# Attention with a gated output projection: VectorE or GpSimd adds the output bias to x

## The chip, the cores and the metric

The kernel runs on one core of one Trainium2 chip. The metric is the device time of one execution in microseconds; the figure compared is the median of several executions. The core has TensorE (PE in the profile), VectorE (DVE), ScalarE (ACT), GpSimd (POOL) and SyncE (SP, here the queue that issues the DMAs).

## What is computed

A model of four layers works on x, 32 sequences of 128 tokens with 128 features in float32. Each layer adds a gated attention and a gated feed-forward to x. Attention has 16 heads of 8 features; queries come from the normalised x, keys and values from a context of the same shape:

```python
x = x + tanh(g_xattn[0]) * attn0(layernorm(x), ctx, mask)
x = x + tanh(g_ffn[0])   * ffn0(layernorm(x))          # fp8 weights and activations
x = x + tanh(g_xattn[1]) * attn1(layernorm(x), ctx)    # ends in  heads @ Wo.T + bo
x = x + tanh(g_ffn[1])   * ffn1(layernorm(x))          # 8 experts, top 2
x = x + tanh(g_xattn[2]) * attn2(layernorm(x), ctx)    # heads attend within one token
x = x + tanh(g_ffn[2])   * ffn2(layernorm(x))
x = x + tanh(g_xattn[3]) * attn3(layernorm(x), ctx, mask)  # ends in  heads @ Wo.T + bo
x = x + tanh(g_ffn[3])   * ffn3(layernorm(x))          # 8 experts, top 2
```

Only layers 1 and 3 have an output projection `Wo` with a bias `bo`. The kernel computes `x + tanh(g) * (heads @ Wo.T)` and adds `tanh(g) * bo`, which is laid out once in `tgbo`, in a second step.

## The kernel before, in words

**Tiles and stages.** x stays in SBUF throughout, as 32 tiles of 128 tokens by 128 features; a tile is one sequence. Four tiles make a group (TG = 4), so there are 8 groups. The kernel is written by hand, engine by engine: every engine has its own program, and semaphores tie them together. The stages follow one another: attention block a = 0, feed-forward 0, attention block a = 1 (layer 1), feed-forward 1, the token attention of layer 2 mixed into it, feed-forward 2, attention block a = 2 (layer 3), feed-forward 3. The start of a block (`start=True`) is mixed into the stage ahead of it.

**Loops.** `walk` (L288) runs a stage's body over the groups: groups 0 and 1 unrolled, groups 2 to 5 in a hardware loop of two trips, groups 6 and 7 unrolled.

**One attention block.** For tile n TensorE writes scores in four banks of four heads (`scores`, L854 the mask, L856 the products), and VectorE takes the row maxima (`head_max`, L1225). Score bank j waits for the maxima of bank j - 2, because only two banks take turns. VectorE splits the maxima in two bf16 parts (L1247, L1249), TensorE turns them (L866), ScalarE copies them (L663), TensorE makes the transposed scores (L875, L879), ScalarE the exponentials (L670), and TensorE weighs the values (L891). The heads are turned (L903), divided by their denominators on VectorE (L1256, L1258), turned again (L908) and multiplied with Wo (L912). The result stands in R_BANK.

**The work around the change.** On VectorE the order inside tile n (all for tile n + 1 or n - 1) is written out by hand in `body`: row maxima of n + 1 (banks 0 and 1), `normalise(n - 1)`, banks 2 and 3, `split_max(n + 1)`, then `add_out(n - 1)`. In the first tile of a group `norm_stats` (L1176, L1181) and `norm` (L1199) of the group after next follow, in the second tile the bias of v (`take_v`, L1210) stands ahead of the row maxima. `add_out` waits for R_BANK, adds gate times R_BANK to x (L1266), waits for that instruction's own semaphore, and adds `tgbo` (L1270), which signals `x_written`.

GpSimd's program in a block (L478 and on) has, per group: `inv_std` for the group after next (L439, L441: variance to rstd, for which VectorE's `norm` waits) and `split` of that group's queries and keys into three bf16 parts (L450, L452, L455). When the split is ready SyncE issues the DMAs that spread the parts over `q_rows` and `k_rows` (L355, L359). `x_written` of a block is waited for by the next stage: by TensorE before its first matmuls, and by VectorE's `norm_stats` for the group at hand.

Of the kernel before, what the change touches and what calls it, by code (L numbers as in the profile page):

```python
# [37 lines left out]
ALU = mybir.AluOpType  # L38
# [3 lines left out]
P = 128  # L42
NT = 32
TG = 4
# [34 lines left out]
def waits_apart(eng):  # L79

    eng.nop(nofuse=True)
# [23 lines left out]
def program(nc, x_in, ctx_in, ctx_t, mask0, mask3, w_attn, w_ffn0, w_router, w_gate, w_up, w_down, w1, w2, gate3,  # L105
            mlp1, mlp2, mlp2_b, cols_in, rows_in, consts_in, pick_in, out):
    with ExitStack() as ctx:  # L107
        def sb(name, shape, dt=F32):
            return ctx.enter_context(nc.sbuf_tensor(name, shape, dt))
# [15 lines left out]
        gates = sb("gates", [P, 8])  # L125
        half_gates = sb("half_gates", [P, 2, 8])
        tgbo = sb("tgbo", [P, 2, P])
# [82 lines left out]
        R_BANK = bank[5]  # L210
# [28 lines left out]
        def tile(n):  # L239
            return x[:, bass.ds(n * P, P)]  # L240
# [16 lines left out]
        R0 = (0, NT, 4 * NT)  # L257
        BLOCK = (0, 2, 5)
        LAYER = (0, 1, 3)
# [28 lines left out]
        def walk(eng, body, chain=None, per_trip=None, after_first=None):  # L288


            body(0, True, False)
            if after_first:
                after_first()
            if chain is not None:
                chain.enter(0, per_trip)
                chain.count = chain.base
            with eng.Fori(0, NG // 2 - 2) as trip:
                if chain is not None:
                    chain.count = chain.base + trip * per_trip
                body(2 + 2 * trip, False, False)  # L300
            if chain is not None:
                chain.leave(NG // 2 - 2)
            body(NG - 2, False, True)
# [4 lines left out]
        def groups(gp, first, last):  # L308

            for b in range(2):  # L310
                yield gp + b, b, first and b == 0, (1 - b if last else 2)
# [3 lines left out]
        def _(sp):  # L315
# [88 lines left out]
            def token_attention():  # L404
                def body(gp, first, last):
                    for gr, b, _, _ in groups(gp, first, last):
                        if positive(TG * (gr - 1)):
                            sp.wait_ge(ctx_tok_read, TG * (gr - 1))
                        waits_apart(sp)
                        sp.dma_start(ctx_tok[b][:], ctx_in[bass.ds(gr * TG, TG)].rearrange("n p d -> p n d")  # L410
                                     ).then_inc(ctx_tok_loaded[b], 16)
                walk(sp, body)
# [18 lines left out]
        def _(pool):  # L431
# [3 lines left out]
            def inv_std(count):  # L435

                pool.wait_ge(stats_ready, count)
                waits_apart(pool)
                pool.tensor_scalar(rstd_a[:], meanvar[:, :, 1], LN_EPS, None, ALU.add).then_inc(pool_steps, ch.one())  # L439
                pool.wait_ge(pool_steps, ch.count)  # L440
                pool.tensor_tensor(rstd[:], rstd_a[:], minus_half[:, 0:TG], ALU.pow).then_inc(rstd_ready, 1)  # L441

            def split(p, a):

                pool.wait_ge(prep_read, 4 * (G0[a] + p) + 3)
                pool.wait_ge(rows_spread, REP * (G0[a] + p))
                for part in range(2):
                    src = qk if part == 0 else qk_rest
                    waits_apart(pool)
                    pool.tensor_copy(parts[:, :, part, :], src).then_inc(pool_steps, ch.one())  # L450
                    pool.wait_ge(pool_steps, ch.count)
                    pool.tensor_tensor(qk_rest, src, parts[:, :, part, :], ALU.subtract).then_inc(pool_steps, ch.one())  # L452
                    pool.wait_ge(pool_steps, ch.count)
                waits_apart(pool)
                pool.tensor_copy(parts[:, :, 2, :], qk_rest).then_inc(split_ready, 1)  # L455
# [20 lines left out]
                walk(pool, body, ch, 12)  # L476

            def attention(a):  # L478
                def body(gp, first, last, a=a):
                    for gr, b, _, left in groups(gp, first, last):  # L480
                        if left >= 2:
                            inv_std(L0[a] + gr + 3)
                            split(gr + 2, a)
                walk(pool, body, ch, 10)

            def feed_forward3():
                def products(k, e):
# [114 lines left out]
            def feed_forward2():  # L602
# [17 lines left out]
                for count in range(46, 51):  # L620
                    inv_std(count)

            todo = (attention0, feed_forward0, lambda: attention(1), feed_forward1_and_tokens,
                    feed_forward2, lambda: attention(2), feed_forward3)
            for step in todo[:PHASES]:
                step()
# [3 lines left out]
        def _(act):  # L630
# [92 lines left out]
            def feed_forward0():  # L723
                def body(gp, first, last):
                    for gr, b, _, _ in groups(gp, first, last):
                        take_turned(0, gr, b)
                walk(act, body, after_first=lambda: attention(1, True))
# [34 lines left out]
            def feed_forward2():  # L762
                take_turned(2, 0, 0)

                def body(gp, first, last):
                    for gr, b, _, left in groups(gp, first, last):
                        for m in range(4):
                            act.wait_ge(hq_filled, 4 * gr + m + 1)
                            act.wait_ge(down_filled, DB2 + gr)
                            waits_apart(act)  # L770
                            act.activation(hq[:, m, :], bank[m][:], ACT.Relu, bias=cols[:, C_B1 + m:C_B1 + m + 1],
                                           saturate=False).then_inc(hq_ready, 1)
                        if left >= 1:
                            take_turned(2, gr + 1, 1 - b)
                        if first:
                            token_exp(NT - TG + b)
                walk(act, body, after_first=lambda: attention(2, True))
# [364 lines left out]
        def _(dve):  # L1142
# [60 lines left out]
            def attention(a, start):  # L1203
# [59 lines left out]

                def add_out(n, a=a):
                    dve.wait_ge(r_filled, R0[a] + 3 * n + 3)
                    ins = dve.scalar_tensor_tensor(tile(n), R_BANK[:, 0:P], gates[:, LAYER[a]:LAYER[a] + 1], tile(n),  # L1266
                                                   ALU.mult, ALU.add)
                    ins.then_inc(r_read, 1)
                    dve.wait_ge(r_read, R0[a] + 3 * n + 3)
                    dve.tensor_tensor(tile(n), tile(n), tgbo[:, a - 1, :], ALU.add).then_inc(x_written, 1)  # L1270

                xc = NT * BLOCK[a]
                if start:
# [36 lines left out]
                def body(gp, first, last, a=a, xc=xc):  # L1310
                    for gr, b, is_first, left in groups(gp, first, last):
                        for t in range(TG):
# [18 lines left out]
                            if has_prev and a > 0:  # L1331
                                add_out(n - 1)
# [12 lines left out]
                if a > 0:  # L1345
                    add_out(NT - 1)
# [387 lines left out]
```

## Time and profile before

| | |
|---|---|
| Three runs, median | 1875.36 us |
| Three runs, lowest and highest | 1872.49 and 1875.47 us |
| The profiled execution, its own time | 1866.39 us |
| Its span, first to last instruction | 1864.6 us |
| TensorE matmuls busy | 1517.3 us, 81% |
| TensorE weight loads busy | 920.6 us, 49% |
| VectorE busy | 1345.4 us, 72% |
| ScalarE busy | 780.6 us, 42% |
| GpSimd busy | 642.2 us, 34% |
| Mean granted TensorE clock | 0.918 |

The busy shares are means over stages that differ in their limits. The two blocks that the edit touches are the stretches from about 403 to 635 us and from about 1365 to 1595 us. Times in the timeline are microseconds from the first instruction. "[2.91 <-DVE neg_max L1225]" behind an instruction says that its engine had stood idle for 2.91 us before it, and what released it. An execution in the loop is told from an unrolled one by its shapes, which the profile then gives once and not as output<-input.

### The profile page before, as it was taken

The page shows a single profiled execution, that of the slowest core. Times are in us where ns is not written, and L with a number is a line of the kernel's source. Part 1 is how long each engine was busy: PE and PEld are TensorE (multiplying, and loading weights), DVE is VectorE, ACT ScalarE, POOL GpSimd, SP SyncE. Part 2 cuts the span into 40 slices and gives each one's busy share as a digit, 9 for nine tenths or more (in the row PEclk, how much of TensorE's full clock was granted, in tenths as well). Part 3 has the DMA queues.
Part 4 walks back from the last instruction along what each step waited for, and adds up shares of the span by engine and source line. Part 5 has one row for each costly group of instructions (what it writes and reads, how often), then busy time and mean ns, then how long its engine had stood idle before and what let it go on. Part 6 is the DMA issues. An engine that isn't in the chain of part 4 may idle for free. (4 is left out here: it accounts for less than half of the span.)

```text
span 1864.6 us, 33511 instructions
## 1 busy us (share of the span) xinstructions
PE 1517.3 (81%) x10824; PEld 920.6 (49%) x10824; DVE 1345.4 (72%) x3512; ACT 780.6 (42%) x1314; POOL 642.2 (34%) x649
## 2 busy tenths in 40 slices
PE   3788885378989799889889898944789899778877
PEld 1455453145555465555555555522355556445444
DVE  5667776666566537888888888876565656698998
ACT  1555563145656423333333433421356556333333
POOL 0223220012221003353444453454123220477786
PEclk9989997589999899999999999975989999798999
DMA  7543540244344000000000000003053432000000
GB/s 171 68 70 47 73 63 1 34 136 74 48 62 62 1 1 1 7 1 7 6 1 6 0 7 18 1 0 74 0 75 46 67 52 36 1 1 12 11 12 12
DMA packets 62835, 63.59 MB, mean 34 GB/s; under 512 B 6065, under 2 KB 57777, under 8 KB 62129
## 3 DMA queue, kind: packets, MB, share of 16 engines
q1 hardware_dynamic: 62704, 61.99, 20.3%
q8 instruction: 66, 1.08, 0.3%
q14 instruction: 65, 0.52, 0.1%
HBM read 22.12 MB, written 2.10 MB: 13 GB/s over the span
## 5 line engine op out<-in xcount | busy, mean ns | idle before, releaser
L1225 DVE TENSOR_REDUCE neg_max<-bank 128x4 f32<-128x512 f32 x384 | 259.5, 687 | 128.9 <-PE bank L856 126.8
L670 ACT ACTIVATE probs<-bank 128x512 f32<-128x512 f32 x384 | 229.1, 597 | 239.1 <-PE bank L879 236.8
L1026 PEld LDWEIGHTS bank<-room,area 128*128 128x128 f32 x2048 | 249.4, 196 | 100.0 <-issue 62.9
L1026 PE MATMUL bank<-room,area 128*128 128x128 f32 x2048 | 259.8, 281 | 32.0 <-DVE area L1499 18.3
L746 ACT ACTIVATE work<-bank 128x512 f32<-128x512 f32 (+1 forms) x192 | 114.5, 596 | 355.0 <-PE bank L1051 349.9
L439 POOL TENSOR_SCALAR rstd_a<-meanvar 128x4 f32<-128x4 f32 x64 | 16.9, 265 | 676.8 <-DVE meanvar L1181 676.8
L854 PE MATMUL bank<-mask_b,ident_b 128*128 128x512 bf16 x384 | 159.4, 415 | 70.5 <-DVE neg_max L1225 56.7
L1055 PE MATMUL bank<-xT,room 128*128 128x512 f32 (+1 forms) x384 | 200.6, 605 | 15.7 <-DVE area L1499 15.5
L1051 PE MATMUL bank<-xT,room 128*128 128x512 f32 (+1 forms) x384 | 198.4, 599 | 0.0
L1499 DVE TENSOR_TENSOR area<-work,bank 128x512 f32<-128x512 f32 (+1 forms) x192 | 128.8, 679 | 94.5 <-PE bank L1055 74.4
L568 POOL TENSOR_TENSOR prod<-mask_i,work 128x128 f32<-128x128 f32 (+3 forms) x128 | 126.4, 1020 | 154.6 <-DVE mask_i L1560 154.6
L856 PE MATMUL bank<-k_rows,q_rows 96*128 96x256 bf16 x768 | 157.3, 288 | 0.0
L879 PE MATMUL bank<-q_rows,k_rows 128*128 128x128 bf16 x1536 | 155.9, 227 | 0.0
L879 PEld LDWEIGHTS bank<-q_rows,k_rows 128*128 128x128 bf16 x1536 | 123.6, 102 | 62.3 <-issue 15.2
L875 PE MATMUL bank<-ident_b,mask_b 128*128 128x512 bf16 x384 | 154.4, 402 | 0.0
L891 PE MATMUL bank<-probs,v_aug 128*32 128x128 f32 x3072 | 151.7, 291 | 1.4 <-ACT probs L670 1.2
L663 ACT ACTIVATE q_rows<-bank 32x512 bf16<-32x512 bf16 x192 | 113.1, 589 | 86.1 <-PE bank L866 82.0
L1470 DVE SCALAR_TENSOR_TENSOR x<-bank,comb,x 128x128 f32<-128x128 f32 (+1 forms) x512 | 143.0, 339 | 4.8 <-PE bank L1026 2.6
L555 POOL TENSOR_TENSOR probs<-h,work 128x128 f32<-128x128 f32 (+3 forms) x128 | 114.4, 923 | 83.1 <-DVE probs L1540 73.8
L1055 PEld LDWEIGHTS bank<-xT,room 128*128 128x128 f32 (+1 forms) x384 | 68.7, 183 | 117.7 <-issue 86.2
L1199 DVE TENSOR_SCALAR xn<-x,meanvar,rstd 128x128 f32<-128x128 f32 (+1 forms) x192 | 76.8, 463 | 55.2 <-POOL rstd L441 55.0
L856 PEld LDWEIGHTS bank<-k_rows,q_rows 96*128 96x128 bf16 x768 | 79.6, 104 | 56.0 <-issue 15.0
(167 smaller groups left out, 2481.9 us busy)
## 6 DMA issues: line engine op xcount, KB each, us to landing
q_rows<-area SPq DMA_DIRECT2D x144, 128.0 KB
k_rows<-area SPq DMA_DIRECT2D x288, 64.0 KB
ctxT<-ctx_t SPq DMA_DIRECT2D x24, 256.0 KB, 7.7
mask_i<-mask SPq DMA_DIRECT2D x8, 256.0 KB, 8.6
work<-ctx_in SPq DMA_DIRECT2D x8, 256.0 KB, 2.8
out<-x SPq DMA_DIRECT2D x4, 512.0 KB, 3.2
room<-w_down SPq DMA_DIRECT2D x1, 1536.0 KB, 13.4
room<-w_gate SPq DMA_DIRECT2D x1, 1408.0 KB, 6.3
```

The costliest lines, as they stand in the source:

```text
L670: act.activation(probs[j].rearrange("p a b -> p (a b)"), T_BANK[j % 2][:], ACT.Exp).then_inc(exp_done, 1)
L854: pe.matmul(dst[:], ident_b[:], bcast(mask(b, t), 4), start=True, stop=False)
L856: mm = pe.matmul(dst[:, 256 * i:256 * i + 256], q_rows[b][SCORE_ROWS, 2 * j + i, tok], k_rows[b][SCORE_ROWS, :, 2 * j + i, tok], start=Fal ...
L875: pe.matmul(dst[:], mask(b, t), bcast(ident_b[:], 4), start=True, stop=False)
L879: mm = pe.matmul(dst[:, i * P:(i + 1) * P], k_rows[b][:, i % 2, 2 * j + i // 2, tok], q_rows[b][:, 2 * j + i // 2, tok], start=False, stop ...
L891: mm = pe.matmul(O_BANK[32 * i:32 * i + 32, j * P:(j + 1) * P], v_aug[b][:, t, 4 * j + i, :], probs[j][:, i, :], start=True, stop=True)
L1026: mm = pe.matmul(dst[:, t * P:(t + 1) * P], h[:, t * P:(t + 1) * P], w, start=i == 0, stop=i == len(terms) - 1)
L1051: pe.matmul(S_BANK[(3 * e + c) % 2][0:size, :], wg[:, e, at:at + size], xT[b][:], start=True, stop=True).then_inc(gate_filled, 1)
L1055: pe.matmul(T_BANK[(3 * e + c) % 2][0:size, :], wu[:, e, at:at + size], xT[b][:], start=True, stop=True).then_inc(up_filled, 1)
L1225: dve.tensor_reduce(neg_max[:, 4 * j:4 * j + 4], S_BANK[j % 2][:].rearrange("p (h k) -> p h k", h=4), AX.X, ALU.max, negate=True).then_inc ...
L1470: ins = dve.scalar_tensor_tensor(xt, src[:, t * P:(t + 1) * P], comb[cb][:, t, e:e + 1], xt, ALU.mult, ALU.add)
L1499: dve.tensor_tensor(hidden[e % 2][0:size, c, :], work[(3 * e + c) % 2][0:size, :], T_BANK[(3 * e + c) % 2][0:size, :], ALU.mult).then_inc( ...
```

## The change

VectorE's `add_out` loses its wait for its own semaphore and the addition of `tgbo`, and its first instruction now signals `r_read` alone. GpSimd gets `add_bias(n)`, which waits until `add_out(n)` has been done, adds `tgbo` to tile n and signals `x_written`. It is called for the four tiles of group g - 1 in the body of group g, behind `inv_std` and `split` where the group has them, and for the last group after the loop. Before its loop GpSimd waits once for `tgbo` to be laid out.

```diff
--- before.py
+++ after.py
@@ -476,12 +476,23 @@
                 walk(pool, body, ch, 12)
 
             def attention(a):
+                def add_bias(n):
+
+                    pool.wait_ge(r_read, R0[a] + 3 * n + 3)
+                    pool.tensor_tensor(tile(n), tile(n), tgbo[:, a - 1, :], ALU.add).then_inc(x_written, 1)
+
                 def body(gp, first, last, a=a):
-                    for gr, b, _, left in groups(gp, first, last):
+                    for gr, b, is_first, left in groups(gp, first, last):
                         if left >= 2:
                             inv_std(L0[a] + gr + 3)
                             split(gr + 2, a)
+                        if not is_first:
+                            for t in range(TG):
+                                add_bias(TG * (gr - 1) + t)
+                pool.wait_ge(setup_dve, 2)
                 walk(pool, body, ch, 10)
+                for t in range(TG):
+                    add_bias(NT - TG + t)
 
             def feed_forward3():
                 def products(k, e):
@@ -1263,11 +1274,8 @@
 
                 def add_out(n, a=a):
                     dve.wait_ge(r_filled, R0[a] + 3 * n + 3)
-                    ins = dve.scalar_tensor_tensor(tile(n), R_BANK[:, 0:P], gates[:, LAYER[a]:LAYER[a] + 1], tile(n),
-                                                   ALU.mult, ALU.add)
-                    ins.then_inc(r_read, 1)
-                    dve.wait_ge(r_read, R0[a] + 3 * n + 3)
-                    dve.tensor_tensor(tile(n), tile(n), tgbo[:, a - 1, :], ALU.add).then_inc(x_written, 1)
+                    dve.scalar_tensor_tensor(tile(n), R_BANK[:, 0:P], gates[:, LAYER[a]:LAYER[a] + 1], tile(n),
+                                             ALU.mult, ALU.add).then_inc(r_read, 1)
 
                 xc = NT * BLOCK[a]
                 if start:
```

## Rows read from the trace of the kernel before

**Rows 1.** The moved line by its own view: count, then ns min/median/max

```profile
L1270 DVE TENSOR_TENSOR x<-x,tgbo x64: 291/292/779, 403.4 to 1595.1; 128x128 f32<-128x128 f32 x32, 128x128 f32 x32
```

**Rows 2.** Busy time by engine in two groups of the second block

```profile
424.22:456.35 32.13, 28.77 (x305) 17.92 (x304) 20.10 (x55) 18.98 (x36) 8.64 (x7) 0.95 0.41 61
521.16:553.75 32.59, 29.11 (x304) 18.50 (x304) 20.11 (x53) 19.08 (x35) 8.63 (x7) 0.95 0.42 56
```

**Rows 3.** Who waited for whom, 403 to 638 us: total, times, longest

```profile
DVE neg_max L1225 <- PE bank L856: 39.8, 68, 1.8
PE bank L854 <- DVE neg_max L1225: 14.4, 5, 2.9
```

**Rows 4.** Timeline, first and second tile of a group: start, us, [idle before]

```profile
521.16 0.35 DVE L1266 SCALAR_TENSOR_TENSOR x<-bank,gates,x 128x128 f32 x1
521.87 0.87 DVE L1176 BATCH_NORM_STATS2 stats<-x 128x6 f32 x4
527.14 0.39 PE L854 MATMUL bank<-mask_b,ident_b 128*128 128x512 bf16 x1 [2.91 <-DVE neg_max L1225]
```

**Rows 5.** Timeline of TensorE, last such gap of the third block

```profile
1522.30 0.61 PE L854 MATMUL bank<-mask_b,ident_b 128*128 128x512 bf16 x1 [2.88 <-DVE neg_max L1225]
```

**Rows 6.** Timeline of VectorE, behind the third tile of that group

```profile
541.49 0.69 DVE L1225 TENSOR_REDUCE neg_max<-bank 128x4 f32<-128x512 f32 x1 [0.19 <-PE bank L856]
```

**Rows 7.** Timeline of VectorE in the last stage

```profile
1705.99 1.12 DVE L1470 SCALAR_TENSOR_TENSOR x<-bank,comb,x 128x128 f32 x4
1707.03 0.86 DVE L1176 BATCH_NORM_STATS2 stats<-x 128x6 f32 x4
```

**Rows 8.** Timeline of VectorE at the end of the third block

```profile
1594.70 0.35 DVE L1266 SCALAR_TENSOR_TENSOR x<-bank,gates,x 128x128 f32<-128x128 f32 x1 [1.58 <-PE bank L912]
1595.29 0.86 DVE L1176 BATCH_NORM_STATS2 stats<-x 128x6 f32<-128x128 f32 x4
```

**Rows 9.** Timeline at the end of the second block

```profile
634.68 0.35 DVE L1266 SCALAR_TENSOR_TENSOR x<-bank,gates,x 128x128 f32<-128x128 f32 x1 [1.28 <-PE bank L912]
635.34 0.30 DVE L1479 MEMSET comb<- 128x128 f32 x2
641.33 1.09 PE L994 MATMUL bank<-ident,xn 128*128 128x128 f32 x4 [6.69 <-DVE xn L1199]
```

**Rows 10.** GpSimd: timeline in one group, then groups of instructions by shape

```profile
512.43 2.13 POOL L452 TENSOR_TENSOR area<-area 128x1024 f32<-128x1024 f32 x1
514.70 1.04 POOL L455 CAST area<-area 128x1024 bf16<-128x1024 f32 x1
523.39 0.23 POOL L439 TENSOR_SCALAR rstd_a<-meanvar 128x4 f32<-128x4 f32 x1 [7.66 <-DVE meanvar L1181]
...
L555 POOL TENSOR_TENSOR probs<-h,work 128x128 f32<-128x128 f32 x32 | 18.8, 589 | 83.1 <-DVE probs L1540 73.8 <-DVE h L1199 9.3
L568 POOL TENSOR_TENSOR prod<-mask_i,work 128x128 f32<-128x128 f32 x32 | 15.2, 476 | 154.6 <-DVE mask_i L1560 154.6
```

**Rows 11.** Timeline of VectorE, third and fourth tile of that group

```profile
539.06 0.17 DVE L1247 CAST neg_max_parts<-neg_max 128x16 bf16<-128x16 f32 x1
546.78 0.46 DVE L1247 CAST neg_max_parts<-neg_max 128x16 bf16<-128x16 f32 x1
```

**Rows 12.** Busy time by engine in short stretches; the clock stands behind POOL

```profile
430.10:433.20 3.10, 3.06 (x19) 1.50 (x20) 1.74 (x4) 0.77 (x2) 0.00 (x0) 0.50 0.56 90
464.10:467.20 3.10, 3.10 (x16) 2.31 (x16) 1.04 (x3) 1.06 (x3) 0.00 (x0) 0.50 0.73 116
597.50:599.50 2.00, 0.00 (x0) 0.00 (x0) 0.87 (x4) 0.28 (x1) 0.00 (x0) 1.00 0.59 113
600.70:603.80 3.10, 3.10 (x20) 1.98 (x16) 0.91 (x2) 1.85 (x4) 0.00 (x0) 0.50 0.01 3
398.20:399.50 1.30, 0.00 (x0) 0.00 (x0) 1.30 (x4) 0.55 (x1) 0.00 (x0) 1.00 0.51 117
399.60:403.00 3.40, 3.37 (x32) 2.26 (x33) 2.58 (x7) 1.40 (x4) 0.00 (x0) 1.00 0.52 119
```

## The prediction

> **What bounds the kernel now.** The whole kernel is eight stages one after the other, so what the edit is worth is read in the two stages that it touches, the second attention block (about 403 to 635 us) and the third (about 1365 to 1595 us). I first read the line that the edit moves. It runs 64 times, 0.292 us in the median [rows 1]; all of them together are about 19 us, which is the most that could go if each stood on the path. Then I read the stage by groups of four tiles. A group lasts 32.13 or 32.59 us, and in it TensorE is busy 29 us and VectorE 20 us [rows 2]: TensorE is the pacemaker and VectorE has room. The waits say the same from both sides. In the second block VectorE waits for score banks 68 times, 39.8 us in all, and TensorE waits for VectorE's row maxima only 5 times, but 2.9 us each [rows 3]. So one place per group is VectorE's and the rest is TensorE's.
>
> The timeline shows which place [rows 4]. In the first tile of a group VectorE finishes tile n-1 with L1266 and L1270, then takes the layer-norm statistics of the group after next (L1176), waits for GpSimd's rstd, normalises (L1199), and only then comes to the bias of v and the row maxima, for whose release TensorE has stood 2.91 us. L1270 is at the head of this chain. In the third block the same gap stands: 2.88 us in its last such group [rows 5]. It follows every L1266 that has an L1176 behind it: 5 groups in each block (groups 1 to 5; group 0 has no tile before it, groups 6 and 7 normalise nothing).
>
> In the other tiles L1270 is followed by a row maximum, and the one after that waits again for TensorE, 0.19 us in the tile shown [rows 6]. Time taken out ahead of such a wait only lengthens it.
>
> **What the edit removes from VectorE.** The wait for the semaphore of the same tile and L1270. L1266 now runs straight into what follows. How close the next instruction can stand to it without a wait is seen in the last stage: four instructions of L1266's kind (L1470, operands of the same shape, one in PSUM) start at 1705.99, take 1.12 us together, and L1176 starts at 1707.03, 1.04 us after the first [rows 7]. That is 0.26 a piece, and I take 0.27 us from L1266's start to L1176's.
> - In the unrolled code the distance from L1266 to L1176 is 0.59 us (1594.70 to 1595.29 [rows 8]): 0.32 us are saved.
> - In the loop it is 0.71 us (521.16 to 521.87 [rows 4]). If the extra 0.12 us belongs to the removed wait, 0.44 us are saved; if it is register work that stays, 0.32 us. I take 0.38, the middle.
> - Each block has one such group in unrolled code (group 1) and four in the loop (2 to 5): 2 x 0.32 + 8 x 0.38 = 3.7 us, with bounds of 3.2 and 4.2.
> - After the last tile of each block the next stage begins with VectorE, and TensorE waits 6.69 us for its normalised tiles [rows 9]. After the second block L1266 to the next instruction is 0.66 us (634.68 to 635.34 [rows 9]), so 0.39 us go; after the third 0.59 [rows 8], so 0.32 go. Together 0.7 us.
> - The other 52 executions (15 in the later tiles of groups 1 to 5, 3 in group 0 and 8 in groups 6 and 7, in each block) stand before a wait for TensorE: 0 us. What covers them is the wait of [rows 6]; were it gone, each would be worth up to its 0.29 us. Eleven of the 64 are lengthened, the longest to 0.779 us [rows 1]; they stand in the fourth tile, where GpSimd's split runs, and there too what comes next is TensorE's.
>
> **What it adds to GpSimd.** 64 additions of 128x128 with both inputs in SBUF. These blocks show none of that size on GpSimd; the nearest rows are the products of a later stage, two kinds of 128x128 multiply at 0.476 and 0.589 us [rows 10]. I take 0.55 us with its wait, 2.2 us for a group of four. They are queued behind the split of the group after next and ahead of the next reciprocal root. The split ends at 515.74 and GpSimd then idles 7.66 us until the statistics come [rows 10]: the four additions fit three times over. Were they slower than 7.66 / 4 = 1.9 us each they would delay rstd, on which VectorE's chain hangs. The tiles they need were finished a group earlier, so their waits are open. Nobody waits for GpSimd's x: the semaphore for a written tile is asked for by the next feed-forward stage alone. In the last group the additions follow tile by tile, and the very last ends some 0.6 us after L1266, while the next stage's first request to GpSimd comes after statistics of 0.86 us at least [rows 8]. Cost 0. No DMA is added or moved: the spreading of the rows waits for the split, and the additions stand behind it, not ahead.
>
> **A rule that speaks against the move.** With the split running, VectorE's cast L1247 takes 0.46 instead of 0.17 us [rows 11] and L1270 up to 0.779 instead of 0.292 [rows 1]: VectorE is held while GpSimd works. The Trainium skill (SBUF — State Buffer, Who interferes with whom) says that a VectorE instruction with two SBUF inputs, or in a two-port mode, and a GpSimd instruction that reads SBUF exclude each other for the whole of one. The trace agrees with it by the two numbers just given. By it the sum would change only if an addition fell on L1247, L1249 or L1199; the block of four would run from 515.8 to about 518 us, and in that stretch VectorE has row maxima out of PSUM. I keep 0.
>
> **The clock.** After each 2.9 us gap TensorE's granted clock falls to the lower of its two levels (1.2 of 2.4 GHz) for 3 us, in half of the groups from the end of the gap, in the others some 1.5 us later. A gap of 2.0 us or more is followed by the low level too, one of 1.3 to 1.5 is not [rows 12]. The edit shortens the gap to about 2.5 us, above the shortest that was punished, so I let the low stretches stand and put 0.
>
> **Sum.** 3.7 + 0.7 = 4.4 us less (3.9 to 4.9 by the bounds). The profiled execution took 1866.39 us (span 1864.6, and 1.8 around it), which would become 1862.0. It lies 9.0 us under the median of the three runs, 1875.36; I take the same saving off the median: **1871.0 us**. About 0.2%, 3.8 us, is what a measurement of this kernel can tell from no change, so the forecast lies just beyond that line.
>
> **Rivals.**
> - **The clock lets go.** A 2.5 us gap lies between those of [rows 12] that were and weren't followed by the low level; how it lies in time also seems to count, since the fall comes at two different distances. A group whose low stretch vanishes gets back about half of 3.1 us, 1.5 us. In five of the ten groups that is 7.5 us on top: 1863.5 us. For: the shortest punished gap is one case. Against: all gaps of 2 us and more were punished.
> - **The clock moves the wrong way.** Groups of 32.13 and 32.59 us alternate [rows 2], and differ in where the low stretch begins. If all ten become the longer kind, five pay 0.46 us: 2.3 us lost of 4.4, 1873.3 us, the same within what can be told.
> - **The head of the chain is not L1270.** If TensorE's own work or a transfer ends the gap a little earlier than VectorE, or the saving is given back later in the group, only the two stage ends remain: 0.7 us, 1874.7 us. Against: the gap is 2.9 us and nothing but VectorE is named in it.
> - **GpSimd is too slow (the slower side).** If an addition took as long as the split's 128x1024 subtraction, 2.13 us by the timeline view of GpSimd [rows 10], four would be 8.5 us, and rstd would be 0.9 us late in each of ten groups, with a hold of 0.3 us on L1247 [rows 11]. That is 12 us lost against 4.4 gained: 1883.0 us. It decides from 1.9 us an addition. Against: half a microsecond for the same size in [rows 10]. The Trainium skill (GPSIMD Engine Reference, Engine selection) advises VectorE for elementwise additions, GpSimd being about twice as slow for two inputs; twice 0.292 is 0.58 us as an estimate from that page, and the trace's 0.476 and 0.589 agree, far from 1.9.
> - **Every execution counts.** If VectorE's time were on the path in all tiles, 64 x 0.33 = 21 us: 1854.3 us. The waits of [rows 3] speak against it.
>
> **Chances.** Forecast 0.50; clock lets go 0.17; clock the wrong way 0.12; saving lost 0.12; GpSimd too slow 0.06; every execution 0.03. Of the forecast's 0.50, a quarter may be measured on the near side of 0.2%. Faster by over 0.2%: 0.38 + 0.17 + 0.03 = 0.58. Within: 0.12 + 0.12 + 0.12 = 0.36. Slower: 0.06. The range reaches from the clock's rival, 1863.5, to 1876.0, which is the case of the lost saving and one microsecond more for the spread of the runs; it leaves out the last two rivals.
>
> **What would show it.** In the changed profile L1266 should be followed by L1176 after about 0.27 to 0.39 us in groups 1 to 5, TensorE's gap before L854 should read about 2.5 us, ten times, and a group should last 31.8 or 32.2 us. In the other tiles VectorE's waits should grow by what L1270 took. GpSimd should show four additions of 0.5 us right behind the split and 5 us of idling behind them. The forecast is wrong if the gap stays 2.9, if low stretches of the clock are missing after some gaps, or if L1247, L1249 or L1199 are longer than now.

## The result, and the profile after

| | before | after |
|---|---|---|
| Median of 13 runs | 1872.49 us | 1862.87 us |
| Lowest and highest | 1863.56 and 1877.55 | 1854.11 and 1868.16 |
| The profiled execution, its own time | 1866.39 us | 1866.35 us |
| Its span | 1864.6 us | 1864.3 us |
| Mean granted TensorE clock in it | 0.918 | 0.919 |

The ratio is 0.9949, with an interval of 0.993 to 0.9968: the changed kernel is 9.6 us faster (6 to 13). The forecast was 4.4 us faster, from a median of 1875.36 to 1871.0 with a range down to 1863.5; the direction held, the size didn't, and the median lies 0.6 us outside the range. The forecast started from the median of three runs; that of 13 is 2.9 us lower, so 2.9 of the 8.1 us by which 1871.0 was missed belong to the starting point.

The two profiled executions took the same time. That is chance, and a warning: the gain is read from the stages, not from the spans.

| Stretch | before | after | difference |
|---|---|---|---|
| Start to first `add_out` of the second block | 403.0 | 405.8 | +2.8 |
| First to last `add_out` of the second block | 231.6 | 224.1 | -7.5 |
| From there to the first `add_out` of the third block | 730.8 | 738.7 | +7.9 |
| First to last `add_out` of the third block | 229.2 | 224.4 | -4.8 |
| From there to the end | 269.9 | 271.3 | +1.4 |

(All in us.) The two blocks together are 12.3 us shorter. The third stretch is made of stages that the edit doesn't touch, but for the end of the second block and the first group of the third, and it measured 729 to 739 us over the profiles of this study, whichever engine added the bias: in this pair it hid the gain.

The page of the changed kernel, parts 1 and 3; engines, then instruction queues:

```profile
PE 1516.6 (81%) x10824; PEld 918.6 (49%) x10824; DVE 1324.7 (71%) x3448; ACT 779.7 (42%) x1314; POOL 669.2 (36%) x713
...
q14 instruction: 69, 0.56, 0.1%
```

VectorE has 64 instructions and 20.7 us less, GpSimd 64 instructions and 27 us more. The line on q14, 65 packets before, matters further down.

Busy time by engine in groups 1 to 5 of the second block, cut at the first tile's `add_out` as in [rows 2]; the clock stands behind POOL:

```profile
427.00:458.90 31.90, 28.86 (x305) 17.98 (x304) 18.75 (x50) 18.98 (x36) 10.29 (x11) 0.95 0.40 61
458.90:489.49 30.59, 27.49 (x304) 17.47 (x304) 18.77 (x50) 18.98 (x35) 10.30 (x11) 1.00 0.43 62
489.49:520.09 30.60, 27.53 (x304) 17.47 (x304) 18.83 (x49) 18.98 (x35) 10.29 (x11) 1.00 0.46 62
520.09:550.71 30.62, 27.50 (x304) 17.47 (x304) 18.78 (x50) 18.98 (x35) 10.29 (x11) 1.00 0.46 60
550.71:581.01 30.30, 27.35 (x304) 17.42 (x304) 18.66 (x50) 18.96 (x35) 11.53 (x14) 1.00 0.46 60
```

This is the result in five lines. Before, each of these groups had a mean clock of 0.95, that is about 3.2 us at the lower level. Now only the first has. The others are 1.5 to 2.0 us shorter each, where the shorter gap alone explains 0.4. In TensorE's own column the same 304 instructions of group 4 are busy 27.5 us instead of the 29.11 of [rows 2]: they weren't fewer, they ran at the higher level. The third block kept two more low stretches (groups 4 and 5), so 3 of 10 are left.

TensorE's timeline, the gap of groups 1, 4 and 5 of that block, as in [rows 4]:

```profile
432.60 0.57 PE L865 MATMUL bank<-mask_b,ident_b 128*128 128x512 bf16 x1 [2.57 <-DVE neg_max L1236]
...
525.70 0.39 PE L865 MATMUL bank<-mask_b,ident_b 128*128 128x512 bf16 x1 [2.52 <-DVE neg_max L1236]
...
556.27 0.39 PE L865 MATMUL bank<-mask_b,ident_b 128*128 128x512 bf16 x1 [2.47 <-DVE neg_max L1236]
```

All ten gaps read 2.47 to 2.57 us, as forecast. The first is followed by an instruction of 0.57 us, at the low level, the others by one of 0.39. In the third block a gap of 2.47 us was followed by the high level once and by the low one once.

VectorE's timeline in the first tile of group 4, then GpSimd's from the end of group 3 to the end of group 4 ([rows 4], [rows 10]):

```profile
520.09 0.35 DVE L1277 SCALAR_TENSOR_TENSOR x<-bank,gates,x 128x128 f32 x1
520.42 0.87 DVE L1187 BATCH_NORM_STATS2 stats<-x 128x6 f32 x4
```

```profile
513.63 1.04 POOL L455 CAST area<-area 128x1024 bf16<-128x1024 f32 x1
514.63 1.70 POOL L482 TENSOR_TENSOR x<-x,tgbo 128x128 f32 x4
521.94 0.23 POOL L439 TENSOR_SCALAR rstd_a<-meanvar 128x4 f32<-128x4 f32 x1 [5.61 <-DVE meanvar L1192]
...
545.28 1.69 POOL L482 TENSOR_TENSOR x<-x,tgbo 128x128 f32 x4
```

L1277 to L1187 is 0.33 us, where L1266 to L1176 was 0.71. GpSimd's four additions stand right behind the split and idle time of 5.6 us follows them, before 7.66.

TensorE's timeline at the end of the second block and of the third:

```profile
636.26 1.09 PE L1005 MATMUL bank<-ident,xn 128*128 128x128 f32 x4 [6.36 <-DVE xn L1210]
...
1599.69 1.09 PE L1005 MATMUL bank<-ident,h 128*128 128x128 f32 x4 [6.72 <-POOL h L513]
```

6.36 us against 6.69 in [rows 9]; the third block's was 7.05 before.

### The profile page after: what moved, and what is told of

It is laid out like the page before. It is cut to its first block and busy times, and to the rows that moved or that the text cites. A ratio compares the mean times of both kernels' runs of the same rounds, so it can differ in the third digit from the quotient of the medians.

```text
span 1864.3 us, 33575 instructions
## 1 busy us (share of the span) xinstructions
PE 1516.6 (81%) x10824; PEld 918.6 (49%) x10824; DVE 1324.7 (71%) x3448; ACT 779.7 (42%) x1314; POOL 669.2 (36%) x713
## 5 line engine op out<-in xcount | busy, mean ns | idle before, releaser
L865 PE MATMUL bank<-mask_b,ident_b 128*128 128x512 bf16 x384 | 156.1, 407 | 67.7 <-DVE neg_max L1236 53.3
L450 POOL CAST area<-area 128x1024 bf16<-128x1024 f32 x36 | 37.3, 1037 | 194.8 <-ACT area L666 192.4
```

The source lines that it names most:

```text
L865: pe.matmul(dst[:], ident_b[:], bcast(mask(b, t), 4), start=True, stop=False)
```

## Experiments

Each ratio sets a kernel beside runs of the kernel before on the same chip, whose medians there were 1870.1 to 1872.3 us; the chips differ from row to row, so the ratios are to be compared and not the medians. "Gap" is TensorE's wait before the mask matmul, in the groups in the hardware loop. "Low groups" are those of the ten (groups 1 to 5 of the two blocks) in which a stretch at the lower clock level follows the gap, counted in one trace of each kernel.

| Kernel | Median, us | Ratio to before | Gap in the loop, us | Low groups |
|---|---|---|---|---|
| before | 1872.49 | 1 | 2.84 to 3.03 | 10 |
| after | 1862.87 | 0.9949 [0.993, 0.9968] | 2.47 to 2.52 | 3 |
| head_only | 1860.62 | 0.9944 [0.9923, 0.9965] | 2.47 to 2.72 | 3 |
| one_column | 1859.67 | 0.9945 [0.9927, 0.9963] | 2.41 to 2.53 | 3 |
| pad_no_wait | 1864.13 | 0.9952 [0.9936, 0.9968] | 2.58 to 2.65 | 7 |
| late_v | 1861.24 | 0.9954 [0.9928, 0.9979] | 1.87 to 1.93, and in 6 of 8 groups 0.62 to 0.64 behind it | 7 |
| small_pad | 1871.6 | 0.9994 [0.9976, 1.0012] | 2.84 to 2.91 | 10 |
| pad_head | 1872.9 | 1.0015 [0.9999, 1.0031] | 2.85 to 2.90 | 10 |

### head_only: the head of the chain alone

From the kernel before, everything stays on VectorE. Only the addition of the tile that is finished in the first tile of groups 1 to 5 is put off by one tile.

```diff
... (`late` leaves the addition out of `add_out`; it is then made by `add_bias`)
                             if has_prev and a > 0:
-                                add_out(n - 1)
+                                add_out(n - 1, late=t == 0 and left >= 2)
+                            if t == 1 and a > 0 and left >= 2 and not is_first:
+                                add_bias(n - 2)
```

> The kernel before, with all additions still on VectorE; only the addition of the tile finished in the first tile of groups 1 to 5 (10 of 64) is moved one tile later, off the head of the chain that leads to the normalisation. Theory A (the change acts through the head of the chain, and through the clock that follows from a shorter gap): TensorE's gap before the mask matmul is about 2.5 us ten times, several low stretches of the clock vanish, and the time is that of the changed kernel, 6 to 13 us less than before (ratio 0.993 to 0.997). Theory B (VectorE's load or its holds by GpSimd count in every tile): 10 of 64 are hardly felt, at most 2 us less.

Measured: 0.9944, the whole gain of the change, with ten additions out of 64 moved and none of them on GpSimd. Gaps of 2.47 to 2.57 us but for one of 2.72, 3 low groups. The place in the code that counts is the one that was forecast.

### pad_head: the head put back

From the changed kernel: VectorE waits again and does an addition that nobody uses.

```diff
                             if t == 0 and left >= 2:
+                                if a > 0 and has_prev:
+                                    dve.wait_ge(r_read, R0[a] + 3 * (n - 1) + 3)
+                                    dve.tensor_tensor(pad[:], wa[:, 0, :], tgbo[:, a - 1, :], ALU.add)
                                 norm_stats(gr + 2, xc - NT + TG * (gr + 3), x_written if a else x_loaded)
```

> The changed kernel, with GpSimd's additions, and one idle addition of 128x128 on VectorE (same wait, same shape, result unused) put back at the head of the chain in groups 1 to 5 of both blocks; 54 of 64 additions stay off VectorE. Theory A: the gap is 2.9 us again, the low stretches come back, and the time is that of the kernel before within 3 us (ratio 0.998 to 1.001), apart from 0.7 us at the ends of the two blocks. Theory B: most of the gain stays, 5 us or more under before.

Measured: 1.0015. Ten instructions of 0.29 us, and their waits, take back everything; the gap is 2.85 to 2.90 and all ten low stretches are there again. GpSimd still does its 64 additions here. Groups 1 to 5 of the second block take 161.4 us, as in the kernel before; those of the third take 163.1 against 161.5, with one low stretch twice as long as the others. So the additions cost nothing that can be seen in the second block, and in the third at most those 1.6 us.

### one_column: what GpSimd's additions cost

```diff
-                    pool.tensor_tensor(tile(n), tile(n), tgbo[:, a - 1, :], ALU.add).then_inc(x_written, 1)
+                    pool.tensor_tensor(tile(n)[:, 0:1], tile(n)[:, 0:1], tgbo[:, a - 1, 0:1], ALU.add).then_inc(x_written, 1)
```

> The changed kernel with GpSimd's additions cut to 1 of 128 columns: the bias is left out on 127 of 128 features. It prices what the additions cost on GpSimd. Theory A: nothing, since GpSimd idles 5.5 us behind them in the changed profile: ratio as for the changed kernel, 0.993 to 0.997. Rival: GpSimd's additions hold VectorE or delay rstd somewhere; then this is faster than the changed kernel by 3 us or more.

Measured: 0.9945 against 0.9949 for the change. What the length of the additions costs is below what these runs can tell, some 3 us.

### late_v: shortening the gap further

```diff
-                            if t == 1 and left >= 1:
+                            if t == 1 and left >= 1 and a == 0:
                                 take_v(gr + 1, 1 - b)
...
+                            if t == 1 and left >= 1 and a > 0:
+                                take_v(gr + 1, 1 - b)
                             if has_prev:
                                 normalise(n - 1)
```

> The changed kernel, and in the two blocks with an output bias the bias of v (0.68 us on VectorE) is put behind the first two row maxima of the second tile, not ahead of them. Theory A: the gap shrinks from 2.5 to about 1.9 us in ten groups, 6 us less, and every low stretch after it goes, about 1.3 us for each group that still has one: groups of 30.0 us, in all 15 to 22 us under before (ratio 0.988 to 0.992). If the clock does not hang on the length of the gap: only the 6 us, about 15 us under before, and the low stretches stay in the trace.

Measured: 0.9954, no gain on the change: a miss. TensorE's timeline of late_v, first and second wait in a group:

```profile
525.90 0.39 PE L865 MATMUL bank<-mask_b,ident_b 128*128 128x512 bf16 x1 [1.92 <-DVE neg_max L1236]
527.59 0.33 PE L919 MATMUL bank<-ident,heads 128*128 128x128 f32 x1 [0.63 <-DVE heads L1269]
```

The 0.6 us that went from the first wait came back after 1.1 us of matmuls: `normalise` now stands behind `take_v`, and TensorE waits for the heads. Both waits together are 2.55 us, as the one of the changed kernel, and 7 groups are low instead of 3. In four of the seven the clock fell 0.2 to 0.9 us after the first wait, before the second began: a wait of 1.9 us alone was followed by the low level, shorter than the 2.0 us of [rows 12].

### small_pad and pad_no_wait: the wait or the addition

Both put something at the head of the chain of the changed kernel: the first keeps pad_head's wait and cuts its addition to 8 columns, the second keeps the full addition and drops the wait.

```diff
+                                    dve.wait_ge(r_read, R0[a] + 3 * (n - 1) + 3)
+                                    dve.tensor_tensor(pad[:, 0:8], wa[:, 0, 0:8], tgbo[:, a - 1, 0:8], ALU.add)
```

```diff
+                                    dve.tensor_tensor(pad[:], wa[:, 0, :], tgbo[:, a - 1, :], ALU.add)
```

> The changed kernel with a smaller idle addition at the head of the chain (8 columns, with the same wait) in groups 1 to 5 of both blocks: the gap should be some 2.7 us, between the changed kernel's 2.5 and the 2.9 of before. If the length of the gap decides whether the clock's low stretch follows, groups without one should be rarer than in the changed kernel (7 of 10) and the time should lie between: ratio 0.996 to 0.999. If the clock has nothing to do with the gap, only 2 us more than the changed kernel and the same number of low stretches.

> The changed kernel with the full 128x128 idle addition at the head of the chain as in pad_head, but without the wait for the semaphore ahead of it. With the wait, 8 columns closed the gap to 2.90 us as 128 columns did. If the wait is what costs in the loop, the gap lies below 2.9, near 2.7 us, in the loop's groups. If the addition's own time costs, it is 2.8 to 2.9. The length of the gap then says again what the clock does: the share of groups without a low stretch and the time should lie between those of the changed kernel and of before, ratio 0.995 to 1.000.

VectorE's timeline of small_pad at the head of the chain, and then that of pad_no_wait:

```profile
518.44 0.35 DVE L1278 SCALAR_TENSOR_TENSOR x<-bank,gates,x 128x128 f32 x1
518.83 0.17 DVE L1345 TENSOR_TENSOR pad<-wa,tgbo 128x8 f32<-128x8 f32 x1
519.15 0.87 DVE L1188 BATCH_NORM_STATS2 stats<-x 128x6 f32 x4 [0.16 <-issue]
```

```profile
518.13 0.35 DVE L1278 SCALAR_TENSOR_TENSOR x<-bank,gates,x 128x128 f32 x1
518.40 0.28 DVE L1344 TENSOR_TENSOR pad<-wa,tgbo 128x128 f32<-128x128 f32 x1
518.60 0.86 DVE L1188 BATCH_NORM_STATS2 stats<-x 128x6 f32 x4
```

small_pad missed its expectation in the loop: an addition a sixteenth as wide, and the distance is 0.71 us as with the full one. pad_no_wait: the full addition, and 0.47 us. Without either it is 0.33. So of the 0.38 us that the edit took away in this group the addition is 0.14 and the wait 0.24. The loop's other two groups, 3 and 5, read 0.29, 0.47 and 0.67: 0.18 and 0.20. In the unrolled group 1 it is the other way round, 0.26, 0.46 and 0.59 us: 0.20 for the addition and 0.13 for the wait. There small_pad's narrow addition did help, with 0.46 us. The wait shows as 0.12 us ahead of the addition and, in small_pad's loop, as 0.16 of "issue" behind it, in which VectorE waits for nothing that the profile names. Why the loop pays more was not tried.

The pair also sets the clock apart. From pad_no_wait to small_pad the gap grows by 0.19 to 0.27 us in the eight loop groups and not at all in the two unrolled ones (2.77 us in both kernels): 1.9 us by addition. The ratios differ by 0.0042, which is 7.9 us (3 to 12 by the two intervals). In the two traces groups 1 to 5 of both blocks differ by 6.1 us, and low groups go from 7 to 10. What is more than proportional is the clock.

### reordered_after, reordered_before, reordered_all: no gap at the head

In the second and the third block (a = 1 and 2 in the code) VectorE's order is changed: the row maxima follow the statistics at once, `norm` comes in the second tile behind `normalise`, and `take_v` already in the first. reordered_before does the same to the kernel before; reordered_all is the changed kernel with the order in all three blocks.

```diff
-                            if t == 1 and left >= 1:
+                            early = a > 0
+                            if t == 1 and left >= 1 and not early:
                                 take_v(gr + 1, 1 - b)
...
+                            if t == 1 and left >= 2 and early:
+                                norm_next(gr, first, b)
                             if has_next:
                                 head_max(n + 1, 2)
+                            if t == 0 and left >= 1 and early:
+                                take_v(gr + 1, 1 - b)
... (`norm_next` waits for rstd and calls `norm`, which no longer stands behind `norm_stats`)
```

> The changed kernel with VectorE's order altered in the two blocks with an output bias: the first two row maxima of the second tile run while GpSimd works on rstd, the normalisation comes behind the division of the heads, and the bias of v one tile earlier. No addition changes its engine. Theory A: TensorE's gap of 2.5 us goes, and no low stretch is left in groups 1 to 5: groups of about 28 us, 30 us or more under the kernel before (ratio 0.980 to 0.986). If the gap only moves to another wait, as when the bias of v was put back, the ratio stays at 0.993 to 0.997.

> The same new order on VectorE, on the kernel before: all additions of the output bias stay on VectorE, tile by tile. Theory A: the additions are no longer at the head of a chain that TensorE waits for, so it is as fast as the reordered changed kernel within 2 us, apart from 0.7 us at the ends of the blocks. Theory B (VectorE's load): it is slower than that one by 8 us or more.

> The reordered changed kernel, with the new order in the first attention block too, whose group lengths have not been looked into. If its gap is of the same kind, another 10 us or more less; if the first block is bound by the loads and the mask, the same time.

Measured: reordered_after 1856.39 us, 0.9927 [0.9908, 0.9947]; reordered_before 1853.6 us, 0.9904 [0.988, 0.9927]; reordered_all 1835.53 us, 0.9827 [0.9801, 0.9854]. The first missed its expectation of 0.980 to 0.986; the second, expected within 2 us of it, is 2.8 us faster by the medians, and not the 8 us slower that VectorE's load would have made it; the third is 21 us under reordered_after, where 10 or more were expected if the first block's gap is of the same kind. TensorE's timeline of reordered_after shows why the first missed:

```profile
493.71 1.10 PE L844 MATMUL bank<-ctxT,wa 128*128 128x512 f32 x2 [2.89 <-DMA ctxT<-ctx_t]
524.28 1.13 PE L844 MATMUL bank<-ctxT,wa 128*128 128x512 f32 x2 [2.59 <-DMA ctxT<-ctx_t]
```

The gap at L865 is gone and a wait for the context's load has taken its place: VectorE was first, the DMA queue second. Both kernels with the new order have lower ratios than both without, though the intervals of reordered_after and of the changed kernel overlap; in the traces groups 1 to 5 of both blocks take 301.8 and 303.9 us with it, 310.7 and 322.9 without. Between the two with the new order the change is worth nothing any more (0.9927 against 0.9904, overlapping, the wrong way round). The gain of the edit hangs on VectorE's chain at the head of the group.

These waits for the context say something of the clock too. The group with the wait of 2.89 us, by its engines, then TensorE in reordered_before and the stretch behind it:

```profile
478.08:508.95 30.87, 27.43 (x304) 17.45 (x304) 18.74 (x49) 18.97 (x35) 10.28 (x11) 1.00 0.46 61
```

```profile
465.13 1.63 PE L833 MATMUL bank<-ctxT,wa 128*128 128x512 f32 x2 [1.71 <-DMA ctxT<-ctx_t]
```

```profile
465.80:468.90 3.10, 3.10 (x24) 1.60 (x22) 1.53 (x3) 1.28 (x2) 1.11 (x2) 0.50 0.00 0
```

A wait of 2.89 us without a low stretch, and one of 1.71 us with one. Over the three traces such waits of 1.4 to 3.2 us were followed by the low level 7 times in 23, and of the twelve from 2.4 to 2.9 us only two were. At the head of the group it was three of ten at 2.5 us, and all ten at 2.84 to 3.03. The length of a wait alone doesn't decide.

### context_first and context_first_before: both limits taken away

SyncE issues the load of the context ahead of the spreading of the rows, which waits for the split; the order on VectorE is that of reordered_all. The second kernel is the same two edits on the kernel before, with the bias on VectorE.

```diff
+                        if left >= 2:
+                            load_ctx(gr + 2, b)
                         if left >= 1:
...
                             spread(gr + 1, 1 - b)
-                        if left >= 2:
-                            load_ctx(gr + 2, b)
```

> The reordered changed kernel (all three blocks), with SyncE's order altered: the load of the context of the group after next is issued ahead of the 18 transfers that spread the rows, not behind them. In the reordered kernels TensorE waits 2 to 3 us per group for this load. Expected: that wait goes, groups fall from 30.5 to about 28.5 us in all three blocks, 25 to 40 us less than reordered_all (ratio 0.960 to 0.970). If the spread is then late instead, TensorE waits for k_rows and the time stays (0.98).

> The same two orders (VectorE's in all three blocks, SyncE's load first) on the kernel before, with the output bias added by VectorE. Theory A: with no gap left at the head of the chain the change is worth 0.7 us at the ends of the blocks and no more; this is within 3 us of context_first. If VectorE's load has become the bound, it is slower than that one by 5 us or more.

Measured: context_first 1814.53 us, 0.9687 [0.9672, 0.9702], as expected; context_first_before 1807.49 us, 0.966 [0.9647, 0.9673], where it was to come within 3 us of the other: a miss. The second is the fastest kernel of the study, 65 us under the kernel before. Busy time by engine in three of its groups, and TensorE's wait in the second:

```profile
433.60:461.41 27.81, 27.26 (x304) 17.46 (x304) 19.90 (x54) 18.97 (x35) 8.64 (x7) 1.00 0.41 63
461.41:490.56 29.15, 27.44 (x304) 17.42 (x304) 20.07 (x54) 18.97 (x35) 8.63 (x7) 1.00 0.53 70
490.56:518.35 27.79, 27.26 (x304) 17.48 (x304) 19.89 (x53) 18.97 (x35) 8.63 (x7) 1.00 0.41 61
```

```profile
476.09 0.39 PE L854 MATMUL bank<-mask_b,ident_b 128*128 128x512 bf16 x1 [0.80 <-DMA k_rows<-area]
```

The gap at the head is gone, and in groups 1 to 5 of both blocks the clock never falls. In the shortest groups TensorE is busy 27.3 of 27.8 us; others, as the second shown, take 28 to 29.5 us, with waits of up to 1 us for the spread rows and for VectorE. Here the change is a loss of 7 us between medians; the ranges of the runs overlap (1808.71 to 1817.06 and 1805.41 to 1812.22), the intervals of the two ratios only touch.

### context_first_1col: where the 7 us are

context_first with one_column's edit.

> context_first with GpSimd's additions cut to 1 of 128 columns (the bias is left out on 127 of 128 features). context_first_before, with the additions on VectorE, was 7 us faster than context_first, which theory A did not expect. If GpSimd's additions themselves cost that (time on its queue, or a hold of VectorE), this comes to about 1808 us (ratio 0.966). If it is something else that goes with the change (the length of the two programs, where the clock's low stretches fall in the stages that the edit does not touch), it stays at about 1814 us (0.969).

Measured: 1813.32 us, 0.9689 [0.9662, 0.9717]. The additions' work on GpSimd isn't it. What differs in the traces of all these kernels lies far from the edit, in the last stage. The changed kernel, VectorE's timeline at about 1734 us, then the kernel before at the same place:

```profile
1734.09 0.19 DVE L1467 TENSOR_TENSOR comb<-route 128x32 f32<-128x32 f32 x1
1737.62 0.75 DVE L1633 TENSOR_SCALAR work<-bank,cols 128x512 f32<-128x512 f32 x1 [3.34 <-issue]
```

```profile
1737.11 0.19 DVE L1459 TENSOR_TENSOR comb<-route 128x32 f32<-128x32 f32 x1
1738.02 0.75 DVE L1625 TENSOR_SCALAR work<-bank,cols 128x512 f32<-128x512 f32 x1 [0.72 <-DVE comb L1459]
```

The DMA view of the changed kernel, 1725 to 1742 us and then 1734.3 to 1737.6 us alone; before, no packet moves from 1725 to 1742:

```profile
q14 instruction: 4, 0.03, 0.7%
...
q14 instruction: 1, 0.01, 1.1%
```

VectorE stands 3.34 us at the turn of its loop, with "issue" and no releaser named, and TensorE waits for it behind (2.75 us at L1118). 2.87 us of it lie right behind the loop's branch; before, 0.25 us do. One packet of instructions arrives in that time, from 1.1 us into it, and the next 0.3 us after its end. The kernels with the bias on VectorE fetch 64 or 65 packets on this queue in all, those with it on GpSimd 68 or 69. The wait of 3.2 to 3.5 us is in all ten traces with the bias on GpSimd, and in none of the four with it on VectorE. From the last `add_out` to the end those four take 269.9 to 270.4 us, mean 270.1; the ten, one_column and context_first_1col among them, 270.9 to 274.7, mean 272.4. The likely reading is that taking the additions out of VectorE's program moved what is loaded at that turn. The Trainium skill (Runtime: NRT & Kernel Launch, Instruction fetch mechanics) says that a taken branch to a page of instructions that isn't loaded has to fetch it before execution goes on; the trace agrees as far as it goes, with the 2.87 us behind the branch and the packet in them, but it doesn't say whose queue q14 is. That the shift of the code is the cause was not tried by itself, by adding instructions elsewhere. The last stage accounts for some 2.3 of the 7 us; the rest stays open. In these two traces the stretch from the last `add_out` of the second block to the first of the third takes 738.2 against 729.2 us (732.7 in context_first_1col), and all that lies ahead of it 4.9 us less; both scatter by as much over the other traces, whichever engine adds the bias.

## Why the prediction was wrong

**What bounds the kernel: right.** One place per group is VectorE's, L1270 stood at its head, and nothing else of it was on the path. head_only (0.9944) and pad_head (1.0015) show both halves.

**The saving in the gap: right to a few hundredths.** The distance fell from 0.71 to 0.33 us in groups 2 and 4 of the loop and from 0.67 to 0.29 in groups 3 and 5 (forecast 0.38 less, measured 0.38) and from 0.59 to 0.26 in the unrolled group (0.32 forecast, 0.33 measured). The 0.38 was the middle between two readings of the loop's extra 0.12 us, and that the middle was hit is luck. That 0.71 held something besides the addition was seen; that in the loop the wait is more than half of the 0.38 was not.

**The ends of the blocks: right.** 0.33 us each, 0.7 forecast for both.

**The other 52 executions and GpSimd: right.** The additions took 0.45 us (0.55 taken) and nobody was held up by them; after the second block the last one was done at 630.9 us, 5.4 us before TensorE's first instruction of the next stage. The rival of a slow GpSimd is gone: the four are done 5.6 us before the statistics come. The Trainium skill (GPSIMD Engine Reference, Engine selection) has GpSimd about twice as slow with two inputs; the trace shows 0.454 against 0.292 us, 1.55 times, for this size. By the Trainium skill (SBUF — State Buffer, Who interferes with whom) an addition could have held VectorE; in the trace no cast L1258 of the two blocks takes over 0.476 us, where L1247 took up to 0.474 before, and 12 casts in each trace are lengthened.

**The clock: the step that failed.** I put this term of the sum at 0, because 2.5 us lay above the shortest gap that had been followed by the low level. It was one case of 2.0 us in another place [rows 12], and I made a threshold of it, with 1.5 us as the next value below. The runs show no threshold of the gap's length: of the ten gaps of 2.47 to 2.57 us three were followed by the low level, of the ten of 2.84 to 3.03 us before all, of pad_no_wait's ten of 2.58 to 2.77 seven, of late_v's ten of 1.9 us seven, and of the twelve waits of 2.4 to 2.9 us for the context two. At the head of the group the share grows with the gap from 2.5 to 2.9 us, in ten groups of one trace each and neighbours of one another, so these shares are rough; what decides in the single case isn't shown. "The clock lets go" was on the list with 0.17 and priced at 1.5 us for each of five groups; it came about in seven, at 1.2 us.

The working of it in the two profiled executions: groups 1 to 5 of both blocks took 161.4 + 161.5 = 322.9 us before and 154.0 + 156.7 = 310.7 after, 12.2 us less. The gaps make 3.9 of that. The other 8.3 are seven groups without a low stretch, 1.2 us each on average; group 3 of the third block is one of them, and it lost 0.9 us to something else (31.5 us, where its like take 30.6). With 0.7 at the ends it is 12.9 us.

**Not on the list: the last stage.** It is about 2.3 us longer by the means of the 14 traces (1.4 in this pair), with VectorE's wait at the turn of its loop. 12.9 - 2.3 = 10.6 us, beside a measured 9.6 (6 to 13). The forecast put everything outside the two blocks at nothing and gave no reason; that the instruction fetch is the cause is argued, not tried.

## What to carry to other kernels

If TensorE has a periodic gap of some microseconds with a low stretch of the clock behind it, price both, and the clock as a chance per gap rather than as a threshold: here 0.4 us off the gap was worth 1.2 us a group on average. Then ask whether the gap has to be there at all: reordering VectorE's chain and the load behind it was worth 65 us, and with it the edit gained nothing. And read a change of half a per cent from the stages and from many runs, since two profiled executions of equal length hid it here.

## What the runs showed of the hardware that was not expected

- A wait of VectorE for its own semaphore between two instructions cost 0.20 to 0.24 us in a loop, more than the addition behind it (0.14 to 0.18), and 0.13 us in unrolled code: distances of 0.33, 0.47 and 0.71 us in a loop's group without either, with the addition alone, and with both. In the loop the same 0.71 us came with an addition of 8 columns as with one of 128.
- The low clock level doesn't follow from the length of a wait of TensorE: it came behind waits of 1.9 us at the head of the group in 7 of 10 groups (late_v) and behind waits of 2.5 us there in 3 of 10 (the changed kernel), and not behind one of 2.89 us in the middle of a group (reordered_after).
- In the ten traces with the bias on GpSimd (three of them with ten idle additions back on VectorE), VectorE stood 3.2 to 3.5 us at the turn of a loop in the last stage, 140 us after the last `add_out`, with nothing but an instruction packet moving; in the four others it didn't, and the kernel's end took 2.3 us less on average.
